# Attention of an image layer on one core: own scores in blocks of eight rows on two banks, relative scores and halves of v and r sums between them

## The reference, cut to what matters

```python
q, k, v = (conv1x1(w, x).reshape(n, 16, 16, 128, 128) for w in (wq, wk, wv))   # n, head, c, row i, pixel
qk  = einsum('nhcij,nhciw->nhijw', q, k) / D
qrq = einsum('nhcij,chjw->nhijw', q, rq) / D
krk = einsum('nhcij,chjw->nhijw', k, rk) / D
weight = softmax(qk + Gq * qrq + Gk * krk, axis=3)        # over j
out = einsum('nhijw,nhciw->nhcij', weight, Gv1 * v) + einsum('nhijw,chjw->nhcij', weight, Gv2 * rv)
```

## Time and profile before

| | us |
|---|---|
| median of 3 runs | 8287.58 (8284.58 to 8298.17) |
| the profiled execution: its own time | 8291.75 |
| its span | 8290.0 |
| TensorE busy | 7187.2 (87%) |
| VectorE busy | 5176.6 (62%) |
| ScalarE busy | 4856.3 (59%) |
| GpSimd busy | 2457.0 (30%) |
| granted clock of TensorE, mean | 0.749 |

### The profile page before, as it was taken

How to read it: one execution, slowest core, us unless ns; L and a number is a source line. 1 busy time by engine, 2 the same in 40 slices (tenths; PEclk the granted TensorE clock), 3 DMA queues, 4 the chain that set the end, 5 groups by cost and what they waited for, 6 DMA issues and landing times. The chain is left out here.

```text
span 8290.0 us, 275612 instructions
## 1 busy us (share of the span) xinstructions
PE 7187.2 (87%) x106442; PEld 6044.4 (73%) x106442; DVE 5176.6 (62%) x20646; ACT 4856.3 (59%) x11427; POOL 2457.0 (30%) x1235
## 2 busy tenths in 40 slices
PE   4999999799999999999999899999999966766738
PEld 3555555689988888898899898898888932332338
DVE  5444444366666666666666666666666768988830
ACT  1444444577777777777777777777777733333410
POOL 0000000243443443444434444434434432322210
PEclk7999999666666666666666666666667688988855
DMA  7555555565655665655556656656656576766522
GB/s 217 203 203 204 204 204 197 113 112 100 112 103 98 113 107 101 107 99 107 101 106 112 102 100 109 109 99 110 105 100 109 92 232 203 265 201 202 208 74 99
DMA packets 1721071, 1148.11 MB, mean 138 GB/s; under 512 B 1143009, under 2 KB 1506145, under 8 KB 1703329
## 3 DMA queue, kind: packets, MB, share of 16 engines
q1 hardware_dynamic: 1530336, 842.56, 48.1%
q10 hardware_dynamic: 188352, 285.27, 9.3%
q0 software_dynamic: 1024, 2.09, 0.1%
HBM read 708.04 MB, written 421.56 MB: 136 GB/s over the span
## 5 line engine op out<-in xcount | busy, mean ns | idle before, releaser
L787 POOL TENSOR_TENSOR att_scores<-att_scores,att_inverse 128x1024 f32<-128x1024 f32 x1024 | 1966.8, 1934 | 2951.7 <-DVE att_inverse L722 2951.7
L660 ACT ACTIVATE att_scores<-att_scores,att_negmax 128x128 f32<-128x128 f32 x8192 | 2509.2, 399 | 67.6 <-issue 67.6
L737 DVE CUSTOM_DVE_ANT_0 att_scores<-att_ps,att_scores 128x128 f32<-128x128 f32 x8192 | 1780.8, 286 | 1066.7 <-PE att_ps L573 957.5
L560 PE MATMUL att_ps<-att_qk,att_rs 32*128 32x64 f32 x32768 | 1793.2, 380 | 155.6 <-ACT att_scores L652 114.2
L560 PEld LDWEIGHTS att_ps<-att_qk,att_rs 32*128 32x128 f32 x32768 | 1698.6, 299 | 196.2 <-ACT att_scores L652 142.5
L573 PE MATMUL att_ps<-att_own 16*128 16x128 f32 x16384 | 1541.6, 405 | 231.3 <-issue 224.1
L573 PEld LDWEIGHTS att_ps<-att_own 16*128 16x128 f32 x16384 | 1416.2, 300 | 268.9 <-issue 264.4
L652 ACT ACTIVATE att_scores<-att_ps 128x1024 f32<-128x1024 f32 x1024 | 992.4, 1021 | 1044.3 <-PE att_ps L560 1044.3
L720 DVE TENSOR_REDUCE att_total<-att_scores 128x8 f32<-128x1024 f32 x1024 | 1233.7, 1205 | 70.7 <-issue 70.7
L594 PE MATMUL att_ps<-att_scores,att_rv 128*16 128x64 f32 x32768 | 1249.6, 334 | 11.0 <-issue 10.8
L594 PEld LDWEIGHTS att_ps<-att_scores,att_rv 128*16 128x16 f32 x32768 | 1193.6, 127 | 24.5 <-issue 13.1
(11 more groups left out here) (146 smaller groups left out, 5276.0 us busy)
## 6 DMA issues: line engine op xcount, KB each, us to landing
qk<-proj_qk_out ACTq DMA_DIRECT2D x64, 2048.0 KB, 8.5
att_qk<-qk SPq DMA_DIRECT2D x512, 256.0 KB, 6.7
att_own<-qk SPq DMA_DIRECT2D x2048, 64.0 KB, 2.5
proj_x<-in_x_dram SPq DMA_DIRECT2D x128, 512.0 KB, 4.3
v_t<-proj_v_out ACTq DMA_DIRECT2D x64, 1024.0 KB, 11.3
att_vt<-v_t SPq DMA_DIRECT2D x128, 512.0 KB, 5.5
att_v<-att_att_v SPq DMA_DIRECT2D x512, 128.0 KB, 4.2
att_r<-att_att_r SPq DMA_DIRECT2D x512, 128.0 KB, 3.5
```

Source lines behind the costliest of these rows:

```text
L560: last = pe.matmul(ps[:, 4 + g, jj * IU:(jj + 1) * IU], rs[32 * g:32 * g + 32, t * JB + jj, :], qk[b][32 * g:32 * g + 32, :, t * JB + jj], ...
L660: last = act.activation(scores[v][:, i, :], scores[v][:, i, :], ACT.Exp, bias=negmax[v][:, i:i + 1], scale=-1.0)
L737: last = dve.tensor_tensor_reduce(out=scores[v][:, i, :], in0=ps[:, 2 * (p % 2) + r // 4, (r % 4) * W:(r % 4 + 1) * W], in1=scores[v][:, i ...
L787: pool.tensor_tensor(scores[v][:, rows, :], scores[v][:, rows, :], inverse[v][:, rows].unsqueeze(2).broadcast_to([P, PR, W]), ALU.mult).th ...
```

## The change

- The own scores use banks 0 and 1 alone; block p starts when all rows of block p-1 have been added. Their matmuls read 32 rows of `own` instead of 16; rows 16 to 31 of each group are cleared once at the start. VectorE signals after each four rows, ScalarE takes exponentials in fours.
- The relative scores use banks 2 to 5, the v sums bank 6, the r sums bank 7.
- TensorE's order: eight steps, each an own block, then at even steps a relative round (rounds 1 to 3 of the next unit, round 0 of the one after), then half a block of v sums and half a block of r sums, of two units ago in the first four steps and of the last unit in the others.
- VectorE alone reads the v sums, ScalarE alone the r sums.
- v is loaded in halves, rv in four strips, `att_v` and `att_r` have two buffers of half the size and are stored in halves; `att_r` in memory has 16 pixels in a row of blocks instead of 32 (`JT`). q and k are loaded ahead of the stores. GpSimd scales the tables at steps 3 and 7 instead of 2 and 4.

```diff
-JT = JG
+JT = JG // 2
+HR = PR // 2
+HALVES = IU // HR
...
             def unit(h, k, u, started, left):
                 if started >= 1:
                     sp.wait_ge(own_done, PIECES * u)
                     load_own(h, k, 1)
-                if started >= 2:
-                    store(*before(h, k, 2), u - 2)
-                if started >= 1:
-                    ph, pk = before(h, k, 1)
-                    later(sp, v_done, FILLS * (u - 1))
-                    load_v(ph, pk)
-                    if pk == 0:
-                        later(sp, r_done, FILLS * (u - 1))
-                        load_rv(ph)
                 if left >= 2:
                     sp.wait_ge(rel_done, ROUNDS * u + ROUNDS)
                     load_qk(*after(h, k, 2))
-                fresh = left >= 2 and k == UPH - 2
+                if started >= 2:
+                    store(*before(h, k, 2), u - 2, 0)
+                if started >= 1:
+                    ph, pk = before(h, k, 1)
+                    later(sp, v_done, FILLS * (u - 2) + FILLS // 2)
+                    load_v(ph, pk, 0)
+                    if pk == 0:
+                        later(sp, r_done, FILLS * (u - 2) + FILLS // 2)
+                        load_rv(ph, 0)
+                        load_rv(ph, 1)
+                fresh = k == UPH - 2 and left >= 2
                 if fresh:
                     load_gain(h + 1)
                     sp.wait_ge(rel_done, ROUNDS * u + ROUNDS + ROUNDS // 2)
                     load_relative(h + 1, 0)
                 if left >= 1:
                     sp.wait_ge(own_done, PIECES * u + PIECES // 2)
                     load_own(*after(h, k, 1), 0)
+                if started >= 1:
+                    later(sp, v_done, FILLS * (u - 1))
+                    load_v(ph, pk, 1)
+                    if pk == 0:
+                        later(sp, r_done, FILLS * (u - 1))
+                        load_rv(ph, 2)
+                        load_rv(ph, 3)
+                if started >= 2:
+                    store(*before(h, k, 2), u - 2, 1)
                 if fresh:
                     sp.wait_ge(rel_done, ROUNDS * u + 2 * ROUNDS)
                     load_relative(h + 1, 1)
...
+            def before_own(u, p):
+                half = p // (PIECES // 2)
                 if p % (PIECES // 2) == 0:
                     pe.wait_ge(own_loaded[half], 128 * u + 128)
-                later(pe, added, PIECES * u + p - 1)
+                later(pe, added, HALVES * u + 2 * p)
+
+            def own_score(u, p, r, gg):
+                half, g, at = p // (PIECES // 2), 2 * (p % 2) + gg, p % (PIECES // 2) // 2 * 4 + r
+                return pe.matmul(ps[:, gg, r * W:(r + 1) * W], own[half][32 * g:32 * g + 32, 1, at, :], own[half][32 * g:32 * g + 32, 0, at, :],
+                                 start=True, stop=True, tile_position=(32 * g, 0))
...
+            def unit(u, v, parts):
+                back2, back1, now, ahead1, ahead2 = parts
+                for p in range(PIECES):
+                    if now:
+                        own_scores(u, p)
+                    if p in (0, 2, 4) and ahead1:
+                        relative(u + 1, v + 1, p // 2 + 1)
+                    if p == 6 and ahead2:
+                        relative(u + 2, v + 2, 0)
+                    if p < 4 and back2:
+                        sums_with_v(u - 2, v - 2, 2 + p // 2, p % 2)
+                        sums_with_r(u - 2, v - 2, 2 + p // 2, p % 2)
+                    if p >= 4 and back1:
+                        sums_with_v(u - 1, v - 1, p // 2 - 2, p % 2)
+                        sums_with_r(u - 1, v - 1, p // 2 - 2, p % 2)
...
+            BEHIND = 2
+
+            def unit(u, v, parts):
+                back2, back1, now, ahead1, ahead2 = parts
+                for p in range(PIECES):
+                    if now:
+                        add_and_largest(u, v, p)
+                    if p % 2 == 1 and p < 4 and back2:
+                        read_v(u - 2, 2 + p // 2)
+                    if p % 2 == 1 and p >= 4 and back1:
+                        read_v(u - 1, p // 2 - 2)
+                    k = p - BEHIND
+                    if k >= 0 and now:
+                        sums_of(u, v, k)
+                    elif k < 0 and back1:
+                        sums_of(u - 1, (v - 1) % BUFS, PIECES + k)
+
+            for half in range(2):
+                dve.memset(own[half][:, :, :, :], 0.0).then_inc(cleared, 1)
+            dve.memset(ps[:, 6:8, :], 0.0).then_inc(cleared, 1)
...
-                        if k == UPH - 2 and not last and p in (2, 4):
-                            scale_relative(h + 1, p // 2 - 1)
+                        if k == UPH - 2 and not last and p == 3:
+                            scale_relative(h + 1, 0)
+                        if k == UPH - 2 and not last and p == 7:
+                            scale_relative(h + 1, 1)
```

More of the change, by code:

```diff
@@ L546, in _, with before_relative @@
+            store(NH - 1, UPH - 2, UNITS - 2, 1)
+            for a in range(2):
+                store(NH - 1, UPH - 1, UNITS - 1, a)
+            for a in range(2):
+                sp.wait_ge(v_stored[a], 64 * UNITS)
+                sp.wait_ge(r_stored[a], 64 * UNITS)
         @block.tensor
         def _(pe):
[L548 removed]
+            def before_relative(u, v, t):
                 if t == 0:
[L550 to L555 removed]
+                    pe.wait_ge(qk_loaded[v % 2], 64 * (u // 2) + 64)
@@ L569, in own_scores @@
+            def own_scores(u, p):
+                before_own(u, p)
                 for r in range(4):
                     for gg in range(2):
-                        g = 2 * (p % 2) + gg
-                        at = block16 * 4 + r
-                        last = pe.matmul(ps[:, g, r * W:(r + 1) * W], own[half][32 * g:32 * g + HD, 1, at, :], own[half][32 * g:32 * g + HD, 0, at, :],
-                                         start=True, stop=True, tile_position=(32 * g, 0))
+                        last = own_score(u, p, r, gg)
@@ L575, in own_scores, with sums_with_v @@
                 last.then_inc(own_done, 1)
-            def sums_with_v(u, v, b, bank):
-                if b == 0:
-                    pe.wait_ge(v_loaded, 16 * u + 16)
-                pe.wait_ge(normed, PIECES * u + 2 * b + 2)
-                for r in range(4):
+            def sums_with_v(u, v, b, half):
+                if half == 0:
+                    if b % (FILLS // 2) == 0:
+                        pe.wait_ge(v_loaded[b // (FILLS // 2)], 16 * u + 16)
+                    if b == 0:
+                        pe.wait_ge(normed, PIECES * u + PIECES)
+                    later(pe, v_read, FILLS * u + b)
+                for r in (2 * half, 2 * half + 1):
@@ L593, in sums_with_r @@
+            def sums_with_r(u, v, b, half):
+                if half == 0:
+                    pe.wait_ge(rv_loaded[b], (u // UPH) * 16 + 16)
+                    later(pe, r_read, FILLS * u + b)
+                for jj in range(half * JB // 2, (half + 1) * JB // 2):
                     for g in range(G):
-                        last = pe.matmul(ps[32 * g:32 * g + HD, bank, jj * IU:(jj + 1) * IU], rv[:, g * JG + b * JB + jj, :], scores[v][:, :, g * JG + b * JB + jj],
+                        j = g * JG + b * JB + jj
+                        last = pe.matmul(ps[32 * g:32 * g + HD, 7, jj * IU:(jj + 1) * IU], rv[:, j, :], scores[v % BUFS][:, :, j],
@@ L640, in _ @@
+            pe.wait_ge(cleared, 3)
             for t in range(ROUNDS):
                 relative(0, 0, t)
+            relative(1, 1, 0)
             units(pe, unit)
@@ L654, in read_relative @@
                 last.then_inc(rel_read, 1)
-            def exp_piece(u, v, p):
-                act.wait_ge(added, PIECES * u + p + 1)
-                for r in range(PR):
-                    i = p * PR + r
-                    last = act.activation(scores[v][:, i, :], scores[v][:, i, :], ACT.Exp, bias=negmax[v][:, i:i + 1], scale=-1.0)
-                last.then_inc(exped, 1)
-            def read_v(u, b, bank):
-                act.wait_ge(v_done, FILLS * u + b + 1)
-                if b == 0:
-                    later(act, v_stored, 64 * u)
-                act.activation(att_v[:, b].rearrange("p r w -> p (r w)"), ps[:, bank, :], ACT.Copy).then_inc(v_read_act, 1)
@@ new lines, in exp_half, with read_r @@
+            def exp_half(u, v, p):
+                act.wait_ge(added, HALVES * u + p + 1)
+                for r in range(HR):
+                    i = p * HR + r
+                    last = act.activation(scores[v % BUFS][:, i, :], scores[v % BUFS][:, i, :], ACT.Exp, bias=negmax[v % BUFS][:, i:i + 1], scale=-1.0)
+                last.then_inc(exped, 1)
+            def read_r(u, b):
+                act.wait_ge(r_done, FILLS * u + b + 1)
+                if b % 2 == 0:
+                    later(act, r_stored[b // 2], 64 * u)
```

(1 more changed line is left out.)

248 lines of the change are left out of this document (76 added, 172 removed).

## The result

The changed kernel took **7892.36 us** in the median of four runs (7884.6 to 7896.67), the kernel before 8286.08 on the same chip (8283.72 to 8298.17). The ratio is 0.9521, with a 95% interval of 0.9505 to 0.9537: 394 us less. The prediction was 8185 with a range of 7960 to 8560.

A forecast was written before the change was run, and what follows sets the result against it. TensorE was taken to bound the attention stage. A unit of 35.8 + 2.0 (instructions) + 1.0 (table) = 38.8 us against 39.7 gave 115 us less over 128 units, plus 10: about 8185 us, range 7960 to 8560.

The forecast's parts named there:

- quiet unit at the full clock: Attention stage: eight steps with switches and own blocks' waits, all at 2.4 GHz, take 34.4 us a unit.
- "issue": TensorE in the attention stage: instructions that come late, 2.0 us a unit kept for the kernel after.
- the price of an own block at the full clock: TensorE's 16 own-score matmuls: 1.12 us at 2.4 GHz, with VectorE beginning about 1.75 us after their start.
- Switches: TensorE changing between row and column blocks: 16 times a unit at 0.25 us each, 4.0 us; ends 0.15 and 0.40.
- the rival by which they eat the gain: Switches at 0.40 us make a unit 2.4 us longer, 8490 us in all; chance 0.16.
- Own blocks' wait for VectorE: Two banks: at odd steps at the full clock an own block waits 0.3 us, four times a unit.
- Waits for ScalarE gone: Relative blocks no longer wait for ScalarE's reading, 0.8 us a unit, having over 8 us to be read.
- The clock: TensorE in the attention stage: granted clock 0.92, fast 84% of the time; ends 0.80 and 1.00.
- the rival of 0.80: The clock does not stay up: at 0.80 the unit is 38.2 us, 8490 in all; chance 0.17.
- The table's wait: Each head's seventh unit: TensorE waits 8 us for the scaled table, 15 heads, 1.0 us a unit; ends 0 and 12.
- The v half: SyncE's queue: the new v half, needed at step 4, lands just in time; 0, upper end 5 us a unit.
- better case: Clock full and no wait for the table: 7870 us, half of it likelier, about 8000; chance 0.15.

The follow-up runs named there:

- ten: Kernel before, with own block 1 next to own block 0, ahead of relative round 0, and the others each one later; one run, 8407.94 us.
- nine: Kernel before, with relative rounds 1 to 3 on TensorE each one own block later; 8344.13 us (1.0077).
- three: Changed kernel, with the first half of v loaded right behind the first own rows, ahead of qk and stores; 7719.00 us (0.9328).

## Why the forecast fell short, step by step

A ledger of a unit, from the forecast's terms to the measured 36.7 us. The clock is used as the prediction used it, with its 45.8 us for a unit at 1.2 GHz, which nothing here measured.

| | us a unit |
|---|---|
| forecast | 38.8 |
| quiet unit at the full clock, 31.1 instead of 34.4 | -3.0 |
| clock 0.91 instead of 0.92 | +0.2 |
| instructions late ("issue"), 153.2 / 127 = 1.2 instead of 2.0 | -0.8 |
| table, 155.9 / 127 = 1.2 instead of 1.0 | +0.2 |
| v halves, 126.3 / 127 = 1.0 instead of 0 | +1.0 |
| left over | +0.3 |
| measured | 36.7 |

(1 / (0.84 / 31.1 + 0.16 / 45.8) = 32.8 against 35.8; with 82% of the time fast, 33.0.)

- **The failed step is the price of an own block at the full clock.** It stands in the sum twice, as the distance to the next block (1.12) and as the time until VectorE can begin to add its rows (1.75). At even steps it was 1.12 us to the next kind and is 0.79: 0.33 too much, four times, 1.3 us a unit. The error was to take a distance between two starts for the price of a block; a copy of VectorE ended just ahead of the second start and fixed it. The copies and the unit without that wait (ten) show this, and the run with rows of 16 excludes the tile's height. At odd steps VectorE's round bounds the step, and there I had 3.5 us, with 1.75 from the start of the own block to VectorE's first addition, brought down from a row at 1.2 GHz. Too little was taken off for the clock: a block of this kernel at 1.2 GHz, from 3553.95, ends after 2.08 us and VectorE begins at 2.28, and at 2.4 GHz, from 3536.13, it ends after 1.16 and VectorE begins at 1.36:

```profile
3537.49 0.30 DVE L726 CUSTOM_DVE_ANT_0 att_scores<-att_ps,att_scores 128x128 f32<-128x128 f32 x1 [0.71 <-PE att_ps L595]
```

  The eight additions then take the 1.7 forecast, and the step is 3.19: 0.31 too much, four times, 1.2 a unit. Together 2.5 of the 3.3 us of the quiet unit, some 290 us over the stage. The profiled execution (7890.68) beat its forecast of 8187 by 296; the other entries of the ledger cancel each other but for a few us, which is luck and not merit of the forecast.
- **Switches.** The quiet pair is 7.47 us without its wait. Own 2 x 0.79, relative 1.87, two halves of v at 0.445 and two of r at 1.15 are 6.64; the 0.83 left over is four switches of 0.21, the two edits that only add switches say 0.15 to 0.19. The prediction had 0.25. In the odd steps VectorE's round hides the difference; the even steps, 4.59 us where 5.09 were forecast, have 0.17 of it in their two switches: 0.7 us a unit too much. That they cost anything was right, and the rival by which they eat the gain falls. The Trainium skill, "TensorEngine Tiling (Array Packing)", Key Properties, has the array drained at a change of tiling mode. The trace agrees with that rule: where kinds of one mode follow each other, the last own matmuls run over the first relative ones (1.05 us from 3531.54, round 1 from 3532.33), and at each change of mode the overlap is no more than 0.08 us.
- **Own blocks' wait for VectorE,** 0.3 at odd steps: right (0.31 and 0.32, 475 waits), but of two terms that were both 0.3 too long, VectorE's round (3.5 for 3.19) and the step (3.2 for 2.87, which is 1.09 + 0.44 + 1.34).
- **Waits for ScalarE gone:** right, 2.4 us.
- **The clock:** 0.92 forecast, 0.91 measured in the stage; the value was right, and the rival of 0.80 falls. That it falls where own and relative blocks meet a wait fits the changed kernel; in the one before it falls without one too (nine).
- **The table's wait:** right in place and size. The wait of the unit shown is 8.27 us for a forecast of 8:

```profile
3567.49 3.69 PE L583 MATMUL att_ps<-att_qk,att_rs 32*128 32x64 f32 x64 [8.27 <-POOL att_rs L759]
```

- **The v half,** put at 0 because it would be just in time: wrong. SyncE's queue in that unit, which starts at 3531.54:

```profile
3529.69 4.68 SPq L477 DMA_DIRECT2D att_own<-qk  x8
3534.66 6.61 SPq L469 DMA_DIRECT2D att_qk<-qk  x4
3541.53 3.95 SPq L493 DMA_DIRECT2D att_v<-att_att_v  x4
3545.57 3.45 SPq L497 DMA_DIRECT2D att_r<-att_att_r  x4
3549.21 0.38 SPq L482 DMA_DIRECT2D att_vt<-v_t  x1
```

  Half the stores cost 7.7 us (3541.53 to 3549.21), not 3.4, as if each store cost by its DMA and not by its bytes, which was the other end of that term. It is no fixed price of a DMA, though: the other half of the same unit's stores took 4.15 us (3563.51 to 3567.66). Own rows (5.0 for 5.8), qk (6.9 for 7.4) and the landing (3.0 for 5.5, since TensorE went on at 3552.23) gave 3.8 back. So the half landed at 20.7 us into the unit, near the 20.2 forecast. It was needed at 18.5, because the steps ahead of it were shorter than forecast: the same error again. Moving the load ahead gave 173 us (three), 1.4 a unit, inside the 5 that the prediction kept as its end.
- **"Issue":** 2.0 us a unit were kept, 1.2 measured. They stand in pairs at one place of a pass of the loop, four units long: in the changed kernel before the own blocks at 3460.28 and 3463.26, at 3615.20 and 3618.50, and at 3757.29 and 3760.72. They are a price of the loop's pass, and not of a unit's order; the additional places that the kernel before has in the middle of its sums (at 3408.72, say) are gone. What exactly TensorE waits for there no run shows.
- **Combine:** 0, about right. The stage explains 391 of the 401 us of span.

The range missed because its lower end took the quiet unit as nearly certain (34.4 us): the better case let only the clock and the table's wait vary. Nothing in it allowed for an own block that was priced too high. That better case gave 7870, close to the 7892 measured, but for a full clock and no wait for the table, and neither came: the nearness is chance. Of the three signs of being wrong, a clock below 0.87, a switch over 0.3 and a wait for v in each unit, none came either (v was waited for 68 times in 127 units); they watched the terms that were thought uncertain, and not the one that failed. What stays open: the 0.3 us a unit left over (half of it, 19 us in all, is short waits for GpSimd's `normalise` and for rv that stand in no entry; the rest isn't shown), and which trait of own and relative blocks the clock goes by.

## What to carry to other kernels

A distance between two starts is a price only if nothing else ends just before the second start: look at every reader of the bank or buffer that the second block writes, since a wait that is shorter than the extent of the block before is not listed as one (some 0.3 us were missing here). When an engine gets faster, recompute when every load of the queue is needed: "just in time" by the old pace is late by the new one, and the order in the one queue decides who pays (v first, then the table, gave 274 us; the table alone 29). Where a block has to wait for another engine's reading, put work of another kind between, even at 0.15 to 0.2 us a switch; without it the same banks cost 19% over the kernel before.

## What the runs showed of the hardware that was not expected

- TensorE's clock fell from 2.4 to 1.2 GHz without a gap in its work in the kernel before with its rounds one block later, the ninth run (a granted 1.00, then 0.65, then 0.50 in three windows that follow each other, with TensorE busy all of the first two and 17.66 of 18.36 us in the third; in the kernel before itself 18.30 us at 0.50, all of them busy), in stretches of matmuls on 32 or 16 rows; it stands at 0.91 to 0.94 with sums on 128 rows between them at every step, and at 0.66 when the same blocks are sorted by kind (that kernel has longer waits too).
- Zeros in 16 more rows of a tile cost no time (0.79 us to the next block with them, 0.78 without), and the granted clock was a little higher with them: 0.71 for 0.68, 0.91 for 0.89.
- A change between row groups and column groups costs 0.15 to 0.21 us at 2.4 GHz on the mean of several; by single distances it is 0.13 to 0.19 from r sums to an own block (1.28 and 1.34 after 1.15), 0.20 from a relative block to v (2.07 after 1.87) and 0.30 from an own block to v (1.09 after 0.79).
- Stores of half the size can take SyncE's queue as long as whole ones: 3.95 us for four of half the size, where four whole ones took 3.18. In the same unit four other halves took 1.89 us (from 3563.51), so the time depends on more than number and size; on what, no run shows.
